# A two-layer window and axial attention kernel: loops written out, two block-diagonal matmuls on 32x32 tiles, v moved to ScalarE, a new software pipeline

## The reference

```python
x = x + _L0_conv_ref(_gn(x), Wq, Wk, Wv, bv, Wo, bo, logit_scale, cpb_w1, cpb_b1, cpb_w2)
x = x + _L1_conv_ref(_gn(x), w_qkv0, w_out0, w_qkv1, w_out1)
```

```python
v = (xw @ Wv.T + bv)
qn = q / jnp.maximum(jnp.linalg.norm(q, axis=-1, keepdims=True), 1e-12)
kn = k / jnp.maximum(jnp.linalg.norm(k, axis=-1, keepdims=True), 1e-12)
logits = jnp.einsum('bhnd,bhmd->bhnm', qn, kn) * scale + 16.0 * jax.nn.sigmoid(bias)
scores = jax.nn.softmax(where(mask, -inf, logits), axis=-1)
z = (scores @ v) @ Wo.T + bo
```

```python
dots = jnp.einsum('bhie,bhje->bhij', q, k) * d ** (-0.5)
out = jnp.einsum('bhij,bhje->bhie', dots, v) @ w_out
```

## Time and profile before

| | us |
|---|---|
| median of three executions | 1061.59 |
| lowest and highest | 1060.19, 1064.38 |
| the profiled execution | 1066.87 |
| its span in the trace | 1064.8 |
| PE, DVE, ACT, POOL busy in it | 969.7, 852.4, 611.9, 458.9 |

### The profile page before, as it was taken

One profiled execution on the slowest core, in us unless ns is written; L12 is line 12 of the kernel. 1 busy time (PEld: TensorE's weight loads), 2 busy tenths in 40 slices (PEclk: granted clock), 3 DMA queues, 4 the chain that ended last, 5 costly groups with the idle time before them and its releaser, 6 DMA issues.

```text
span 1064.8 us, 43208 instructions
## 1 busy us (share of the span) xinstructions
PE 969.7 (91%) x18068; PEld 832.4 (78%) x18068; DVE 852.4 (80%) x1684; ACT 611.9 (57%) x881; POOL 458.9 (43%) x329
## 2 busy tenths in 40 slices
PE   2468999999999989999899998999899999999874
PEld 2347888888888878888788987888788888888763
DVE  3658889888888888888788996888788888888841
ACT  2336566666666655666665664666456665666531
POOL 4123455344445453454444543454444444544430
PEclk9879999999999999999999998999999999999997
DMA  5102333333333332333333332333323333333332
GB/s 162 38 1 42 50 49 58 52 47 48 61 55 60 62 56 40 54 49 60 56 58 59 55 53 36 57 57 61 58 45 55 47 58 58 56 52 52 47 49 48
DMA packets 432682, 57.51 MB, mean 54 GB/s; under 512 B 413268, under 2 KB 431974, under 8 KB 432486
## 3 DMA queue, kind: packets, MB, share of 16 engines
q1 hardware_dynamic: 432486, 54.65, 31.2%
HBM read 12.63 MB, written 8.40 MB: 20 GB/s over the span
## 4 chain that ended last, share of the span: by engine, by line
PE 60%; SPq 11%; issue 9%; DVE 6%; POOL 4%; ACT 4%; DMA 4%; POOLq 0%; ACTq 0%; DVEq 0%
PE ps L439 27%; PE ps L626 6%; PE ps L649 4%; SPq L382 4%; PE ps L666 4%; PE ps L517 4%; SPq L390 3%; PE ps L472 3%; PE ps L550 3%; DMA gram_wide<-gram 3%; PE ps L650 2%; PE ps L532 2%; POOL kv L955 2%; PE ps L490 2%; PE ps L718 1%
## 5 line engine op out<-in xcount | busy, mean ns | idle before, releaser
L955 POOL TENSOR_TENSOR kv<-kv,kv 128x1024 f16<-128x1024 f32 x64 | 152.4, 2381 | 156.4 <-ACT kv L798 156.4
L798 ACT ACTIVATE kv<-kv 128x1024 f16<-128x1024 f32 x64 | 87.9, 1374 | 115.8 <-DVE kv L1114 115.8
L439 PE MATMUL ps<-xn,w_q 128*128 128x256 f16 x1152 | 143.7, 274 | 8.7 <-issue 8.7
L439 PE MATMUL ps<-xn,w_k 128*128 128x256 f16 x1152 | 144.7, 276 | 4.5 <-issue 4.0
L955 POOL TENSOR_TENSOR xn<-xn,xn 128x512 f16<-128x512 f32 x64 | 74.7, 1166 | 162.3 <-ACT xn L828 162.3
L960 POOL TENSOR_TENSOR stat<-stat,small 128x2 f32<-128x2 f32 x64 | 44.1, 690 | 207.3 <-DVE stat L1093 207.3
L439 PEld LDWEIGHTS ps<-xn,w_q 128*128 128x128 f16 x1152 | 111.2, 98 | 24.8 <-issue 11.6
L439 PEld LDWEIGHTS ps<-xn,w_k 128*128 128x128 f16 x1152 | 109.2, 99 | 20.0 <-issue 5.0
L626 PEld LDWEIGHTS ps<-v_wide,k_wide 128*128 128x128 f16 x3072 | 100.7, 98 | 29.9 <-issue 17.5
L649 PE MATMUL ps<-q,gram_wide 128*128 128x32 f16 x2048 | 111.5, 177 | 13.4 <-DMA gram_wide<-gram 13.4
L649 PEld LDWEIGHTS ps<-q,gram_wide 128*128 128x128 f16 x2048 | 108.2, 97 | 17.6 <-DMA gram_wide<-gram 16.8
(11 more groups left out here) (110 smaller groups left out, 1928.0 us busy)
## 6 DMA issues: line engine op xcount, KB each, us to landing
k_wide<-kv SPq DMA_DIRECT2D x256, 64.0 KB, 2.3
gram_wide<-gram SPq DMA_DIRECT2D x512, 32.0 KB, 2.4
x_in<-x SPq DMA_DIRECT2D x32, 128.0 KB, 2.5
x_in<-x SPq DMA_DIRECT2D x64, 64.0 KB, 2.5
out<-y_out SPq DMA_DIRECT2D x32, 128.0 KB, 2.3
out<-y_out SPq DMA_DIRECT2D x64, 64.0 KB, 2.5
probs<-L_conv_w_qkv SPq DMA_DIRECT2D x1, 768.0 KB, 6.8
x<-L_conv_w_qkv SPq DMA_DIRECT2D x1, 768.0 KB, 8.5
```

The source lines that it names most:

```text
L439: last = pe.matmul(dst, w[:, wp, c, m * P:m * P + P], act[:, xp, c * TOK:(c + 1) * TOK], start=(n == 0), stop=(n == 5))
L798: act.activation(halves(kv[a][:], 0), kv32[a][:].rearrange("p t n -> p (t n)"), ACT.Copy).then_inc(kv_hi[a], 1)
L955: return pool.tensor_tensor(dst, whole, high, ALU.subtract)
```

## The change

- `Fori` goes: all steps are written out, and all awaited counts are constants. `edge` waits are written for the first and last eight images.
- `window_norms` and `group_means` multiply only the four 32x32 tiles on the diagonal, since `head16` and `group8` are zero outside them: four matmuls on 32 rows and 32 columns each take the place of one on 128x128, into the same bank, at different partitions.
- `spread_v` goes from DVE to ACT and adds no bias. As the softmax sums to one, bv passes through Wo as a constant: twelve one-column matmuls and two ACT instructions make `bo_col` from it once, before the first `window_out`.
- Every engine's step has a new order. The pipeline has one step more in all (PE has 37 steps instead of 36), `scores(0)` and `scores(1)` are apart, and all PSUM banks are dealt anew with other waits for them.

The core of the diff (the `edge` and `reach` lines for the new banks are left out):

```diff
-            for k in range(peeled):
-                step(0, k)
-            with eng.Fori(0, loops) as i:
-                for u in range(UNROLL):
-                    step(i, peeled + u)
-            for k in range(peeled + UNROLL * loops, IMAGES + stages - 1):
-                step(0, k)
+            for k in range(IMAGES + stages - 1):
+                step(k)
...
                 for t in range(2):
-                    last = pe.matmul(ps[:, NORM_BANK + t, :], head16[:], qk_sq[:, t, :], start=True, stop=True)
+                    for q in range(4):
+                        rows = slice(32 * q, 32 * q + 32)
+                        last = pe.matmul(ps[rows, NORM_BANK + t, :], head16[rows, rows], qk_sq[rows, t, :],
+                                         start=True, stop=True)
...
-                    last = pe.matmul(ps[:, GM_BANK[layer], 0:6].rearrange("p (g v) -> p g v", v=3), group8[:],
-                                     halves[:, :, h, :], start=(h == 0), stop=(h == 1))
+                    for q in range(4):
+                        rows = slice(32 * q, 32 * q + 32)
+                        last = pe.matmul(ps[rows, GM_BANK[layer], 0:6].rearrange("p (g v) -> p g v", v=3),
+                                         group8[rows, rows], halves[rows, :, h, :], start=(h == 0), stop=(h == 1))
...
+                if is_first(img):
+                    pe.wait_ge(bv_hi, 1)
+                    pe.wait_ge(bv_lo, 1)
...
+                    last.then_inc(bo_proj, 1)
+                    pe.wait_ge(bo_ready, 1)
...
-                        last = dve.scalar_tensor_tensor(dst[:, :, DH * b:DH * b + DH], src[:, :, b, :], 1.0 / WS,
-                                                        add[:, :, b, :], ALU.mult, ALU.add)
+                        last = act.activation(dst[:, :, DH * b:DH * b + DH], src[:, :, b, :], ACT.Copy, scale=1.0 / WS)
...
-        QK_BANK, NORM_BANK, V_BANK, DEN_BANK, PV_BANK, Z_BANK = 0, 4, 5, 1, 3, 7
-        S_BANK, KV_BANK, Q_BANK = (6, 0), (3, 3), (5, 2)
-        G_BANK, O_BANK, GM_BANK = (4, 6), (0, 6), (2, 3)
-        Y_BANK, YT_BANK, XT_BANK = 2, 5, 3
+        QK_BANK, NORM_BANK, V_BANK, DEN_BANK, PV_BANK, Z_BANK = 6, 4, 7, 1, 2, 3
+        S_BANK, KV_BANK, Q_BANK = (4, 4), (0, 2), (6, 3)
+        G_BANK, O_BANK, GM_BANK = (2, 0), (4, 6), (0, 0)
+        Y_BANK, YT_BANK, XT_BANK = 1, 6, 5
```

More of the change, by code:

```diff
@@ L56, in missing @@
 def missing(n):
-    return isinstance(n, int) and not 0 <= n < IMAGES
+    return not 0 <= n < IMAGES
 def reach(eng, sem, img, per=1, j=None):
@@ L754, in step @@
[L754 to L763 removed]
+                for img in there(k - 1):
+                    scores(1, img)
+            over_steps(step, 6)
         @block.scalar
@@ L895, in result_copy, with step @@
                                ACT.Copy).then_inc(y_copied, 1)
-            def step(i, c):
-                for img in there(i, c):
-                    image_copy(img)
-                for img in there(i, c - 1):
+            def step(k):
+                for img in there(k - 3):
+                    kv_high(0, img)
+                for img in there(k - 1):
+                    squares(img)
+                for img in there(k - 4):
+                    o1_high(1, img)
+                for img in there(k - 1):
@@ new lines, in step @@
+                for img in there(k - 2):
+                    o_high(img)
+                for img in there(k - 4):
+                    o1_side(0, img)
+                for img in there(k - 1):
+                    qk_high(img)
+                for img in there(k - 3):
+                    gram_high(1, img)
+                for img in there(k - 2):
+                    window_bias(img)
+                for img in there(k - 4):
+                    o1_high(0, img)
+                for img in there(k - 3):
+                    q1_high(0, img)
@@ new lines, in step @@
+                for img in there(k):
+                    image_copy(img)
+                for img in there(k - 3):
+                    gram_high(0, img)
+                for img in there(k - 1):
+                    spread_v(img)
+                for img in there(k - 5):
+                    result_copy(img)
+                for img in there(k - 2):
+                    normed_high(1, img)
+                for img in there(k - 3):
+                    o1_side(1, img)
+                for img in there(k):
+                    normed_high(0, img)
@@ L942, in _ @@
+                for img in there(k - 1):
+                    probabilities(1, img)
+                for img in there(k - 2):
+                    kv_high(1, img)
+                for img in there(k - 1):
+                    probabilities(0, img)
+            over_steps(step, 6)
         @block.gpsimd
@@ new lines, in step @@
+            def step(k):
+                for img in there(k - 5):
+                    add_x1(img)
+                for img in there(k - 1):
+                    group_var(0, img)
+                for img in there(k - 2):
+                    add_bias(1, img)
+                for img in there(k - 1):
+                    group_norm(0, img)
+                for img in there(k - 4):
+                    o1_sum(1, img)
+                for img in there(k - 3):
+                    turn(1, img)
+                for img in there(k - 2):
+                    add_bias(0, img)
+                for img in there(k - 3):
+                    turn(0, img)
+                    widen_v(1, img)
+                for img in there(k - 2):
@@ L1273, in step @@
+                for img in there(k - 4):
+                    o1_sum(0, img)
+                for img in there(k - 3):
+                    gram_low(1, img)
+                for img in there(k - 2):
                     add_x(img)
                     group_stats(1, img)
-            over_steps(dve, step, 5)
+                for img in there(k - 3):
+                    q1_low(0, img)
+                for img in there(k - 2):
+                    group_moments(1, img)
+                for img in there(k - 1):
+                    mask_k(img)
@@ L1281 @@
+                for img in there(k - 2):
+                    group_var(1, img)
+                for img in there(k):
+                    group_stats(0, img)
+                for img in there(k - 2):
+                    group_norm(1, img)
+                for img in there(k):
+                    group_moments(0, img)
+                for img in there(k - 3):
+                    gram_low(0, img)
+            over_steps(step, 6)
 _INS = ["x", "L0_conv_Wq", "L0_conv_Wk", "L0_conv_Wv", "L0_conv_bv", "L0_conv_Wo", "L0_conv_bo",
```

438 lines of the change are left out of this document (196 added, 242 removed).

## The result

The changed kernel is slower than the kernel before by 0.6%, not faster by 2%:

| | before | changed |
|---|---|---|
| median, us | 1064.01 | 1069.72 |
| lowest and highest, us | 1059.04, 1071.69 | 1064.13, 1075.74 |
| ratio, 95% interval | | 1.0056 [1.0035, 1.0077] |
| the profiled execution (span), us | 1066.87 (1064.8) | 1067.31 (1065.5) |

The account below looks back on a forecast made before the run. PE's own work, 29.10 us of a 30.48 us step, was taken as the floor. Steps -15.7, start -3 and end -3 made -21.7 us, giving 1040 us after taking 5.3 us off to the median; range 1022 to 1062.

Parts of the forecast that it names:

- The loop: Writing out the step loop removes PE's issue pauses (14.2 us) and the low clock after them (6 us): -20 us.
- rival 2: The pauses belong to the long program, not the loop, and come again elsewhere: 1060 us, chance 0.08.
- The tiles: Head norms on 32x32 tiles run four at once, 1.72 us plus 0.1; group means stay at 0.44 us.
- Rival 4: Diagonal tiles run one after another, norms 6.9 us, 5.2 us more a step: 1206 us, chance 0.04.
- Place (1): Norms behind q and k: PE waits for the squares, queued behind `kv_high(0)` on ACT, 0.35 us a step.
- Place (2): Axis 1's gram chain through eight DMAs, 10.1 to 11.1 us against 10.6 of work: 0.25 us wait at `axial_out(1)`.
- The start: Before the 27 steps: second image's statistics come later, `scale_qk` 4.9 us earlier; net -3 us (+3 to -8).
- The end: After the 27 steps: gram1 and gram0 in one step, last axial outputs close together; -3 us (+3 to -8).
- Rival 3: Place (2)'s DMA chain becomes the bound at 13 to 14 us, step 32.5 us: 1110 us, chance 0.08.

Follow-up runs that it names:

- e1: The kernel before with only its loop written out (edge waits for the first and last eight images): 1039.58 us, 0.9770 of the kernel before.
- e3: The changed kernel with head norms and group means on the full 128x128 array again, no tiles: 1072.36 us, 1.0067 of the kernel before.
- e6: The changed kernel with gram 1 ahead of `axial_out(0)` on PE, and ACT's and DVE's halves moved up likewise: 1050.13 us, 0.9871 of the kernel before.
- e5: The changed kernel with only four of axis 1's eight `gram_wide` DMAs, half of that axis's result missing: 1037.63 us, 0.9745 of the kernel before.
- e9: The changed kernel with four of axis 1's eight `gram_wide` DMAs issued by ACT instead of SP: 1053.96 us, 0.9896 of the kernel before.
- e10: e8 with four of axis 1's eight `gram_wide` DMAs issued by ACT, as in e9: 1050.21 us, 0.9860 of the kernel before.
- e7: The changed kernel with DVE's `group_moments(1)` ahead of `q1_low(0)`: 1068.38 us, 1.0027 of the kernel before.
- e8: The changed kernel with the moves of e6 and e7, and the squares ahead of `kv_high(0)` on ACT: 1048.76 us, 0.9854 of the kernel before.

## Why the prediction was wrong

I predicted 1040 us with a chance of 0.80 for faster; it was 1069.7. Against the profiled execution of before I had -21.7 us, and it was +0.7. By its steps:

- **The loop, -20 us: right.** e1 measured 25 us. It was 26.2 us in the steps, for the short waits that I had put down to others went with it: e1's step is 29.51, and 29.10 + 0.41 of waits, where I had kept 0.65. The 1.00 in its row, for all 27 steps, has one stretch of low clock left in it, at 104.1 us. The pauses did not come again (rival 2 is out).
- **The tiles, +0.1 us each: right, and worth nothing.** Norms 1.85 us (1.72 + 0.1 forecast). Rival 4 would have had 6.9. The Trainium skill says on "TensorEngine Tiling (Array Packing)", in "Restrictions and Gotchas", that different row tiles cannot access the same PSUM bank at once; the row of L472 disagrees, for tiles that write different partitions of the bank. The means took 0.24 us instead of 0.44, so PE's own work per step stayed at 29.07, not 29.3: 6 us in the kernel's favour that I had not counted, and that were waited away.
- **Place (1), the squares: mechanism right.** In the trace PE stands 0.18 us a step there instead of 0.35, with the norms' load standing 0.6.
- **Place (2), the DMA chain of axis 1: the step that failed.** I set 10.1 to 11.1 us against 10.6 us of work, and took a wait of 0.25. The chain took 11.3 us in the step shown: 1.5 for ACT, 1.4 for DVE, 6.04 for eight issues, 2.3 from the last issue's end to PE's start. ACT and DVE came as charged. The mis-sized term is the eight DMAs: 7.0 to 8.0 us in my sum, 8.4 here. I charged seven issues and took the last's landing from its start; over the 27 steps the eight take 5.3 to 6.7 us, and 2.1 to 3.7 pass from there. The 0.66 us an issue that I took from the earlier trace rows were the first four of a group of eight, whose sixth took 1.5 us. And I took a mean issue and a median landing, but PE waits for the last of eight, in every step anew: a step with slack gives nothing to the next, so the mean of the wait lies above the wait of the mean. The work that hides the chain was about as long as charged: 10.3 us of blocks and 0.35 us of wait for the moments. The wait was 0.63 us and not 0.25.
- **What hangs on it, which I had not counted at all: low clock** behind the longest waits, 0.31 us a step with the first stretch and 0.25 without it. I knew such a clock loss from the loop's pauses and booked it as the loop's alone. The 27 steps of before have as much of it, 17.0 us at 1.2 GHz, as those of the changed kernel: the pauses' share went, and this came.
- **A third place, missed: the moments of layer 1**, 0.35 us a step at L733, on PE's path between gram 1 and `axial_out(1)`. While the DMA chain is the bound, this wait only takes the place of one at `axial_out(1)`, as e3's added work did; with the chain out of the way it is the next bound (e6). The new order made part of it. Ahead of the moments DVE adds `x<-z,x_t`, two instructions, which took 0.76 us before and take 1.74 now, with an instruction of POOL under way beside them (before, then changed):

```profile
490.88 0.76 DVE L1211 TENSOR_TENSOR x<-z,x_t 128x256 f32<-128x256 f32 x2 [1.48 <-ACT z L876]
...
582.51 1.74 DVE L1247 TENSOR_TENSOR x<-z,x_t 128x256 f32<-128x256 f32 x2
582.68 1.29 POOL L1001 TENSOR_TENSOR o<-o,o 128x512 f16<-128x512 f32 x1 [0.46 <-ACT o L841]
```

  In all 27 steps of before each of the two takes 0.42 to 0.43 us, with POOL idle. Now the first takes 0.40 to 0.44 us and the second 1.38 to 1.42, with POOL's instruction beside it for 1.1 us. That is 1.0 us more a step against 0.35 of wait, and about what DVE's work fell short of the 54 us. No run kept the two apart, so that the wait would go with it is argued, not shown.
- **Sum of the step:** 29.07 + 0.18 + 0.35 + 0.63 + 0.31 = 30.54, beside 30.49 measured, against 29.9 forecast. That is 16 of the 22.4 us.
- **The start, -3: right.** `bias_mask` on DVE started at 32.90 us, and `scale_qk` at 37.36 instead of 44.58:

```profile
32.90 4.42 DVE L1106 TENSOR_TENSOR bias_mask<-v_wide 128x64 f32<-128x64 f32 x32 [2.93 <-DMA v_wide<-position_table]
37.36 0.87 DVE L1205 SCALAR_TENSOR_TENSOR qk<-qk_sq,q_cap,ps 128x256 f32<-128x256 f32 x2
```

  Both are 2.3 to 2.4 us earlier than forecast. The first transposes of the 27 steps start at 96.88 us, as before (96.87), with norms and gram 1 (3.2 us of PE's work) already done: 3.2 us gained.
- **The end, -3: the wrong sign.** It took 145.6 us against 144.9, with those 3.2 us less left to do and one `result_rows` (0.5 us) more: 3.4 us worse. Without other images beside it PE stands for the last `gram_wide` bare (waits from 919.87 us on):

```profile
PE ps L662 <- DMA gram_wide<-gram: 10.9, 4, 3.8
PE ps L637 <- DMA k_wide<-kv: 4.5, 2, 4.0
```

  I had written that the chain is not shorter, and still booked a gain. Against the changed kernel e5 gave back 7.2 us there, e9 4.0 and e10 3.5. The clock of the changed kernel is lower there than that of before, too: 0.90 against 0.94. Which part of the end's loss is the order and which the DMAs is not settled.

Rival 3 named the mechanism, place and turning point (slower from a wait of 1.05 us at `axial_out(1)`), but only in a large form, 1110 us at 0.08. The 0.63 us of direct wait is below that point, and the kernel was slower all the same, for the clock, the moments and the end stood beside it.

Why the order before did not have this wait: its tightest stretch of the kind is axis 0's. In e1, which keeps that order (PE, start, duration):

```profile
566.11 1.47 PE L432 MATMUL ps<-xn,w_q 128*128 128x256 f16 x12
...
575.40 2.78 PE L659 MATMUL ps<-o,w_o 128*128 128x256 f16 x24
578.02 0.18 PE L642 MATMUL ps<-q,gram_wide 128*128 128x32 f16 x1
```

From the end of gram 0 (566.11) to `axial_out(0)` (578.02) stand 11.9 us without a wait, where the change leaves 10.8. e6 adds 1.6 to these 10.8 and has no DMA wait left in its steady steps. The order before has 1.1 us more for its chain than the new one, and that is more than the mean wait; that it is this and nothing else in the two orders is argued from these rows, and no run changed it alone.

## What to carry to other kernels

Write a loop out, or change an order, but not both in one go: here the first gave 25 us and the second took 30. Where a chain passes through several DMAs that one queue issues one after another, charge all the issues, the last one's landing at its late end, and give it a microsecond of slack beyond that; a wait that recurs in each step doesn't average out. Count work removed between two ends of such a chain as worth nothing, and follow every pause of PE to the clock behind it. When a move makes one wait shorter, look at what it made later: e7 and e8 traded a wait for the moments for one of the same size.

## What the runs showed of the hardware

- A DMA issue on SP took 0.63 us in the median, but 0.585 to 1.958 over the 512 of `gram_wide`; in each group of eight none to two took over 0.9 us, in the kernel before as in the changed one. Four issues on ACT (e9) held that engine for 3.0 to 4.6 us. The row is of the changed kernel:

```profile
L381 SPq DMA_DIRECT2D gram_wide<-gram x512: 585/630/1958, 95.7 to 1046.4; - x171
```

- In the changed kernel, waits of 0.9 to 1.95 us on a PE that was otherwise busy were followed by 3.4 us at 1.2 GHz in four cases, and in a fifth with another wait just before; two of 1.0 us (that end at 345.9 and 897.0 us) were not. Nor does the length of a wait alone decide it: in e7 waits of 1.36 and 1.39 us (at 381.1 and 502.6 us) were not followed by low clock, in e9 one of 0.65 us was.
- Sixteen f32 records on 32x32 tiles of different rows, into one bank, took 1.85 us: the 1.72 of four on 128x128, and 0.13 more.
- VectorE's add of two f32 operands in SBUF, 128x256, took 0.42 us with POOL idle and 1.38 to 1.42 us with POOL's instruction on 128x512 beside it for 1.1 us.
